# A graph layer and a mixture of experts on one core: block numbers loaded elsewhere, one-hots made a step ahead, W3's split moved, the expert loop written out

## What is computed

```python
def _L0_gnn_ref(x, edge_index, edge_attr, W1, b1, W2, b2, W3, b3, W4, b4, gamma, beta):
    src, dst = (edge_index[0], edge_index[1])
    edge_feat = jnp.concatenate([x[src], x[dst], edge_attr], axis=-1)
    h = mish(edge_feat @ W1 + b1)                # mish(x) = x * tanh(softplus(x))
    messages = mish(h @ W2 + b2)
    agg = jax.ops.segment_sum(messages, dst, num_segments=x.shape[0])
    u = mish(jnp.concatenate([x, agg], axis=-1) @ W3 + b3)
    y = x + (u @ W4 + b4)
    mu = jnp.mean(y, axis=-1, keepdims=True)
    var = jnp.mean(jnp.square(y - mu), axis=-1, keepdims=True)
    return (y - mu) * jax.lax.rsqrt(var + LN_EPS) * gamma + beta

def _L0_ffn_ref(hidden_states, gate_weight, w1, w2):
    gate_logits = x @ gate_weight.T
    top_vals, top_idx = jax.lax.top_k(gate_logits, 2)
    routing_w = jax.nn.softmax(top_vals, axis=-1)
    h = jax.nn.silu(jnp.einsum('td,efd->tef', x, w1))
    h_mean = jnp.einsum('tef,te->ef', h, mask) / counts[:, None]   # per expert
    y_mean = jnp.einsum('ef,edf->ed', h_mean, w2)
    return jnp.einsum('tk,tkd->td', routing_w, y_mean[top_idx])

x = x + _L0_gnn_ref(_layernorm(x), edge_index, edge_attr_64, ...)
x = x + _L0_ffn_ref(_layernorm(x)[None], gate_weight, w1, w2)[0]
```

## Time and profile before

| | us |
|---|---|
| median of 3 runs | 1254.94 (1253.52 to 1257.24) |
| the profiled execution | 1255.11 |
| its span, first to last instruction | 1253.5 |
| PE, DVE, ACT, POOL busy | 1084.6, 958.0, 837.7, 713.5 |
| mean granted TensorE clock | 0.929 |

### The profile page before, as it was taken

One profiled execution on the slowest core, in us unless ns is written; L12 is line 12 of the kernel. 1 busy time (PEld: TensorE's weight loads), 2 busy tenths in 40 slices (PEclk: granted clock), 3 DMA queues, 4 the chain that ended last, 5 costly groups with the idle time before them and its releaser, 6 DMA issues. The chain is left out here.

```text
span 1253.5 us, 19768 instructions
## 1 busy us (share of the span) xinstructions
PE 1084.6 (87%) x5651; PEld 884.2 (71%) x5652; DVE 958.0 (76%) x1678; ACT 837.7 (67%) x1025; POOL 713.5 (57%) x574
## 2 busy tenths in 40 slices
PE   3993999999999999999999999996389985668974
PEld 2772788787778778878777877885267764658862
DVE  6651799898989989989989999998548875733366
ACT  3212889989988998998998988897045441523342
...
GB/s 167 276 89 153 143 121 130 125 125 125 129 126 122 127 128 121 129 126 123 129 125 126 124 126 129 119 149 1 23 46 42 33 58 82 205 76 127 134 130 179
DMA packets 129763, 148.72 MB, mean 119 GB/s; under 512 B 73253, under 2 KB 81862, under 8 KB 129597
## 3 DMA queue, kind: packets, MB, share of 16 engines
...
## 5 line engine op out<-in xcount | busy, mean ns | idle before, releaser
L907 PE MATMUL ps<-W2h,w1l_w3l 128*128 128x512 f32 x1264 | 426.6, 398 | 0.0
L778 POOL DMA_INDIRECT gath<-dst_table,idx_sl x158 | 265.2, 1679 | 48.6 <-issue 47.1
L771 POOL DMA_INDIRECT gath<-src_table,idx_sl x158 | 207.9, 1316 | 126.1 <-PE ps L902 86.0
L907 PEld LDWEIGHTS ps<-W2h,w1l_w3l 128*128 128x128 f32 x1264 | 227.3, 189 | 38.6
L907 PE MATMUL ps<-W2l,w1l_w3l 128*128 128x512 f32 x632 | 248.2, 393 | 0.0
L845 DVE TENSOR_TENSOR agg<-agg,ps 125x512 f32 x166 | 114.0, 687 | 76.5 <-issue 47.7
L785 POOL TENSOR_TENSOR msg_lo<-act,msg_hi 128x512 fp32r<-128x512 f32 x79 | 144.2, 1825 | 35.3 <-DVE msg_hi L891 35.3
L907 PEld LDWEIGHTS ps<-W2l,w1l_w3l 128*128 128x128 f32 x632 | 119.0, 188 | 27.2
L802 ACT ACTIVATE act<-ps 128x1024 f32<-128x1024 f32 x79 | 81.2, 1027 | 74.8 <-PE ps L939 74.8
L902 PE MATMUL ps<-ident,gath 128*128 128x128 f32 x632 | 99.0, 282 | 34.8 <-DVE agg L845 18.4
L902 PEld LDWEIGHTS ps<-ident,gath 128*128 128x128 f32 x632 | 73.6, 142 | 62.5 <-DVE agg L845 35.3
...
## 6 DMA issues: line engine op xcount, KB each, us to landing
...
```

The source lines that it names most:

```text
L771: pool.indirect_dma_start(out=gath[:, k, j, :], out_offset=None, in_=src_table[:, :], in_offset=bass.IndirectOffsetOnAxis(ap=idx_sl[:, p % ...
L778: pool.indirect_dma_start(out=gath[:, k, j, :], out_offset=None, in_=dst_table[:, :], in_offset=bass.IndirectOffsetOnAxis(ap=idx_sl[:, p % ...
L907: return nc.tensor.matmul(ps_2[:, p % 2, j, :], part[:, p % 2, d, j * P:(j + 1) * P], weights[:, d, :], start=False, stop=last)
```

## The change

Four things are changed.

1. In the edge stage `value_load` is taken out of `add_sums`. The number for the first addition is loaded behind the second activation's product (L875 before) and ahead of L879, that for the second addition behind the lo part of h (L884) and ahead of L887, so L887, L891 and L852 now stand between it and the addition.
2. The one-hot at that place in VectorE's order is that of f = s - 3 instead of m = s - 4, in three buffers (OH) instead of two.
3. W3's lo parts: VectorE makes four (0 to 3), one each in the steps PAIRS + 4 to PAIRS + 7, GpSimd four (4 to 7) in step PAIRS + 3. Before, VectorE made six, two each in PAIRS + 2 to PAIRS + 4, and GpSimd two.
4. The expert loop is written out for all 35 tiles on every engine. `row_sl` and `carrier` are gone, the gathers take their rows from `row_i` directly, and `xg` has four buffers (XG). The routing weights (`weights()`) are computed ahead of the loop. `reach`, `hs` and `spread_hm` lie on the memory of `bias_r`, which the expert stage does not read.

The edge stage's part of the diff, and the buffers:

```diff
         act_parts = {PAIRS: (0, 1, 2, 3), PAIRS + 1: (4, 5, 6, 7)}
-        dve_parts = {PAIRS + 2: (0, 1), PAIRS + 3: (2, 3), PAIRS + 4: (4, 5)}
-        pool_parts = {PAIRS + 3: (7, 6)}
+        dve_parts = {PAIRS + 4: (0,), PAIRS + 5: (1,), PAIRS + 6: (2,), PAIRS + 7: (3,)}
+        pool_parts = {PAIRS + 3: (4, 5, 6, 7)}
         hi_order = act_parts[PAIRS] + act_parts[PAIRS + 1]
...
-            def add_sums(p, j):
-                b = dve.value_load(block_i[0:1, p * 2 + j:p * 2 + j + 1], min_val=0, max_val=BLOCKS - 1)
+            def visit_block(p, j):
+                return dve.value_load(block_i[0:1, p * 2 + j:p * 2 + j + 1], min_val=0, max_val=BLOCKS - 1)
+
+            def add_sums(p, j, b):
                 row = agg[:, bass.ds(b, 1), :].rearrange("p a d -> p (a d)")
                 dve.wait_ge(S["sum_ps"], p + 1)
                 if p * 2 + j > 0:
...
                 if visited(o):
-                    add_sums(o, 1)
+                    add_sums(o, 1, second)
...
-                if visited(m):
-                    if m >= 2:
-                        dve.wait_ge(S["sum_ps"], m - 1)
-                    nc.vector.tensor_tensor(onehot[:, m % 2], iota_n[:].unsqueeze(1).to_broadcast([P, 2, NE]),
-                                            dloc[:, 2 * m:2 * m + 2].unsqueeze(2).to_broadcast([P, 2, NE]), ALU.is_equal).then_inc(S["onehot_ready"], 1)
+                if visited(f):
+                    if f >= OH:
+                        dve.wait_ge(S["sum_ps"], f - OH + 1)
+                    nc.vector.tensor_tensor(onehot[:, f % OH], iota_n[:].unsqueeze(1).to_broadcast([P, 2, NE]),
+                                            dloc[:, 2 * f:2 * f + 2].unsqueeze(2).to_broadcast([P, 2, NE]), ALU.is_equal).then_inc(S["onehot_ready"], 1)
...
+                if visited(m):
+                    first = visit_block(m, 0)
                 if exists(p):
                     dve.wait_ge(S["exp1"], p + 1)
                     nc.vector.tensor_scalar(a1, a1, EXP_MAX, 1.0, ALU.min, ALU.add).then_inc(S["inc1"], 1)
                 if visited(m):
-                    add_sums(m, 0)
+                    add_sums(m, 0, first)
                 if exists(r):
                     dve.wait_ge(S["h_hi"], r + 1)
                     nc.vector.tensor_tensor(hTl[:, r % 2], h, f32(hTh[:, r % 2]), ALU.subtract).then_inc(S["h_lo"], 1)
+                if visited(m):
+                    second = visit_block(m, 1)
...
                     o = sums(m)
                     for j in range(2):
                         for lo, part in enumerate((msg_hi, msg_lo)):
-                            ins = nc.tensor.matmul(o[0:NE, j, :], onehot[:, m % 2, j, :], part[:, bass.ds(slots[j], 1), :].rearrange("p a n -> p (a n)"),
+                            ins = nc.tensor.matmul(o[0:NE, j, :], onehot[:, m % OH, j, :], part[:, bass.ds(slots[j], 1), :].rearrange("p a n -> p (a n)"),
...
-        carrier = sb("f_carrier", [1, 2])
-        row_sl = sb("row_sl", [P, 2, 1], I32)
-        xg = sb("xg", [P, 2, HID])
+        xg = sb("xg", [P, XG, HID])
...
-        hs = sb("hs", [P, 2, FFN])
+        hs = over_bias("hs", [P, 2, FFN], 0)
```

The expert loop's part (ScalarE's is rewritten in the same way):

```diff
-            def step(i, c):
-                g, k, _ = tile(i, c + 2)
-                if within(g, RT):
-
-                    pool.wait_ge(S["row_ready"], g + 1)
-                    need(pool, S["xgT_ps"], g - 1)
-                    pool.wait_ge(S["carried"], g + 1)
-
-                    nc.gpsimd.tensor_tensor(carrier[:, 0:1], carrier[:, 1:2], carrier[:, 1:2], ALU.add).then_inc(S["carried"], 1)
-                    pool.indirect_dma_start(out=xg[:, k, :], out_offset=None, in_=xl_scr[:, :],
-                                            in_offset=bass.IndirectOffsetOnAxis(ap=row_sl[:, k, 0:1], axis=0)).then_inc(gathered[k], 16)
-
-            nc.gpsimd.memset(carrier[:], 0.0).then_inc(S["carried"], 1)
-            steps(pool, step, FIRST, LAST, LO, HI, UNROLL)
+            pool.wait_ge(S["rows_ready"], 1)
+            for t in range(RT):
+                if t >= XG:
+                    pool.wait_ge(S["xgT_ps"], t - XG + 1)
+                pool.indirect_dma_start(out=xg[:, t % XG, :], out_offset=None, in_=xl_scr[:, :],
+                                        in_offset=bass.IndirectOffsetOnAxis(ap=row_i[:, t:t + 1], axis=0)).then_inc(gathered[t % XG], 16)
...
-            def step(i, c):
-                g, k, used = tile(i, c + 3)
-                if within(g, RT):
-
-                    need(dve, gathered[k], used * 16)
-                    nc.vector.tensor_copy(row_sl[:, k, :], row_i[:, bass.ds(g, 1)]).then_inc(S["row_ready"], 1)
-                if isinstance(i, int) and c == FIRST + 1:
-
-                    weights()
-                m, km, _ = tile(i, c - 3)
-                if within(m, RT):
-
-                    e = dve.value_load(expert_i[0:1, bass.ds(m, 1)], min_val=0, max_val=E - 1)
+            weights()
+            for t in range(-1, RT + 3):
+                m, n = t - 3, t + 1
+                if m >= 0:
+                    e = dve.value_load(expert_i[0:1, m:m + 1], min_val=0, max_val=E - 1)
                     cols = hsum[:, :, bass.ds(e, 1)].rearrange("p f a -> p (f a)")
                     dve.wait_ge(S["sum_ps"], m + 1)
                     need(dve, S["summed"], m)
-                    nc.vector.tensor_tensor(cols, cols, ps_s[:, km, 0:FC], ALU.add).then_inc(S["summed"], 1)
-                n, kn, _ = tile(i, c + 1)
-                if within(n, RT):
-
+                    nc.vector.tensor_tensor(cols, cols, ps_s[:, m % 2, 0:FC], ALU.add).then_inc(S["summed"], 1)
+                if n < RT:
                     dve.wait_ge(S["xgT_hi"], n + 1)
-                    nc.vector.tensor_tensor(xgTl[:, kn, :], ps_t[:, kn, :], f32(xgTh[:, kn, :]), ALU.subtract).then_inc(S["xgT_lo"], 1)
-
-            steps(dve, step, FIRST, LAST, LO, HI, UNROLL)
+                    nc.vector.tensor_tensor(xgTl[:, n % 2, :], ps_t[:, n % 2, :], f32(xgTh[:, n % 2, :]), ALU.subtract).then_inc(S["xgT_lo"], 1)
...
-            def step(i, c):
-                t, k, _ = tile(i, c)
-                if within(t, RT):
-                    e = pe.value_load(expert_i[0:1, bass.ds(t, 1)], min_val=0, max_val=E - 1)
-                n, kn, used = tile(i, c + 1)
-                if within(n, RT):
-
-                    pe.wait_ge(gathered[kn], used * 16 + 16)
+            for t in range(-1, RT + 2):
+                m, n = t - 2, t + 1
+                if 0 <= t < RT:
+                    e = pe.value_load(expert_i[0:1, t:t + 1], min_val=0, max_val=E - 1)
+                if n < RT:
+                    pe.wait_ge(gathered[n % XG], (n // XG + 1) * 16)
                     need(pe, S["xgT_lo"], n - 1)
                     for q in range(KC):
-                        ins = nc.tensor.transpose(ps_t[:, kn, q * P:(q + 1) * P], xg[:, kn, q * P:(q + 1) * P], ident[:])
+                        ins = nc.tensor.transpose(ps_t[:, n % 2, q * P:(q + 1) * P], xg[:, n % XG, q * P:(q + 1) * P], ident[:])
                     ins.then_inc(S["xgT_ps"], 1)
-                m, km, _ = tile(i, c - 2)
-                if within(m, RT):
-
+                if 0 <= m:
                     pe.wait_ge(S["h_act"], m + 1)
                     need(pe, S["summed"], m - 1)
                     for f in range(FC):
-                        ins = nc.tensor.matmul(ps_s[:, km, f:f + 1], hs[:, km, f * P:(f + 1) * P], valid[:, bass.ds(m, 1)], start=True, stop=True)
+                        ins = nc.tensor.matmul(ps_s[:, m % 2, f:f + 1], hs[:, m % 2, f * P:(f + 1) * P], valid[:, m:m + 1], start=True, stop=True)
                     ins.then_inc(S["sum_ps"], 1)
-                if within(t, RT):
-
+                if 0 <= t < RT:
+                    k = t % 2
...
-
-            steps(pe, step, FIRST, LAST, LO, HI, UNROLL)
-
```

36 lines of the change are left out of this document (17 added, 19 removed).

## The result

The changed kernel takes **1197.4 us** (median of 4 runs, 1195.2 to 1197.9) against 1254.5 us: ratio 0.954, 95% interval 0.952 to 0.956. Predicted were 1200, range 1192 to 1214. The profiled execution took 1197.5 us, its span is 1195.9, so the trace of before (span 1253.5) and this one differ by 57.6 us.

The account below looks back on a forecast made before the run. The prediction took VectorE to set the edge stage's period, partly by fetching block numbers while TensorE waits. Its terms, -34 - 11 - 10 = -55, gave 1200 us from a profiled 1255.11, range 1192 to 1214.

Parts of the forecast that it names:

- Term 1: Edge stage: moving the two block number loads ends TensorE's 0.50 us wait per period; -34 us, bounds -36 and -24.
- The witness periods: Edge stage: the last two periods with gathered tiles, at 8.98 us, taken as the period after the change.
- the 1 us for hiccups: Edge stage: taken off 35 us for small hiccups that count fully once TensorE is the bound.
- The witnesses named: Edge stage signs: period 8.98 to 9.0, no VectorE wait or issue time before additions; load above 0.9 us means upper bound.
- The upper bound of 0.15 us a period: Edge stage: a slow load behind L884 sticks out of its 1.22 us cover by 0.15 us at most.
- Terms 2 and 3: Drain: one-hots a step ahead -9.4, W3's split -2.3, one hold +1; together -11 us, bounds -14 and -5.
- The 1 us charged for one more held operation: Drain: GpSimd's doubled W3 parts would hold a VectorE operation once more; 1 us.
- Term 4: Expert loop: no copies or carrier, four buffers, tiles 2.33 us apart instead of 2.66; -10 us, bounds -11.5 and +0.
- Another limit at 9.2 us or more: Rival, edge stage: a gather, ScalarE or GpSimd holds the period at 9.2 to 9.25; 1217 us, chance 0.12.
- A starving written-out loop: Rival, expert loop: seven instruction refills at 1.5 us each use up the 10 us; 1210 us, chance 0.08.
- The drain gives nothing: Rival, drain: GpSimd's parts hold VectorE throughout; 1206 to 1211 us, chance 0.04.
- Loads that wait for everything ahead of them: Rival, edge stage: both loads stick out fully wherever they stand, period 9.99 us; 1270 us, chance 0.03.

Follow-up runs that it names:

- a1: The kernel before with only the two block number loads moved behind the long products: 1220.5 us, ratio 0.972.
- a2: The changed kernel with each block number load put back right ahead of its addition: 1231.4 us, ratio 0.981.
- a3: The changed kernel with the second load one place further back, behind the messages' hi part (0.69 us): 1198.3 us, ratio 0.954.
- a4: The kernel before, loads unmoved, with GpSimd's half of msg_lo ahead of its gathers of the second table, which start later: 1219.3 us (one run).
- c3: The changed kernel with GpSimd's W3 parts waiting for VectorE's last msg_lo, and GpSimd's msg_lo ahead of the second table's gathers: 1195.0 us, ratio 0.952.
- b3: The kernel before with only the one-hots a step ahead, in three buffers: 1246.2 us, ratio 0.994.
- b4: The changed kernel with W3's split as before, six parts on VectorE and two on GpSimd: 1199.8 us, ratio 0.956.
- b1: The kernel before with only the written-out expert loop and its four gather buffers: 1244.1 us, ratio 0.991.
- b2: The changed kernel with two gather buffers in place of four, the expert loop still written out: 1203.3 us, ratio 0.959.
- a5: The changed kernel with VectorE's block numbers of the edge stage replaced by constants, so no load is left there: 1194.4 us, ratio 0.952.

## Why the prediction was right, and where its steps were not

- **Term 1, the loads, -34.** Measured -34.9 (after), -35.3 (a1), +34.0 (a2). The witness periods without gathers, 8.98 us, gave the right period for the ones with gathers, and the 1 us for hiccups was not needed. The witnesses named all hold: issue time before additions gone but for 0.4 us, loads below 0.9 us. The *reason* was half right. "I cost both loads at nothing where they land" rested on cover; a3 and a4 show that the loads are short there because they no longer meet the second adding gather, and c3 shows for the first load that cover hides a held one too (for the second, behind L889, no run shows it). The prediction named the gather as running beside the slow load, and took its witness from it, but didn't ask beside which gather the moved loads would land. That they land where a load is short was not foreseen, and in so far luck. The upper bound of 0.15 us a period was never touched.
- **Terms 2 and 3, the drain, -11 (-9.4, -2.3, +1).** Measured -11.9. One-hots alone 9.0 (b3), the split 2.9 to 3.4 (after against b3, b4 against after), where -2.3 + 1 was put. A step was put at "some 2.4 us, about what TensorE's four matmuls take"; it is 2.23, and VectorE's alone: TensorE's clock was granted at its higher level from about 848.5 us, behind two sums that ran back to back (a sum's matmul then shows 0.40 instead of 0.63 us), and it waits 1.0 us a step. The 1 us charged for one more held operation is the step that was wrong: held in the drain after are the last msg_lo (1.75 us) and the one-hot ahead of it (1.11 at 842.06), and both stand in the trace of before too (1.75 at 879.01, 1.12 at 869.98), so the change added none. TensorE's first sum came 1.9 us earlier (41.4 for 43.3 behind pair 77), where 2.3 was put, and the steps with one part instead of two are shorter by the rest.
- **Term 4, the expert loop, -10.** Measured -11.9 by the table, of which 0.8 is the clock at the start, so -11.1 from the fourth tile on (b1's medians: -10.7). The undisturbed tile was 2.33 in the earlier trace rows and is 2.30, so that 31 tiles give 11.1 us where 10.2 was put; the 0.5 us for the first gather are 0.4; the 0.7 us for fetching the longer program have no counterpart in the trace: 30 tiles run at 2.30 us without one exception. The prediction didn't say what share the buffers have; b2 shows 7.5 us for them and 3.0 to 3.6 for the copies, the carrier and the loop on the chip.
- **The rivals.** Another limit at 9.2 us or more: no, TensorE is busy in every microsecond of the stage. A starving written-out loop: no; the queue of instruction fetches moved 49 packets where there were 44, and no tile pauses. By the Trainium skill's rule that the prediction quotes (Runtime: NRT & Kernel Launch, Instruction fetch mechanics) refills are mostly hidden, and the trace agrees: tiles 2.30 us apart throughout. The drain gives nothing: no. Loads that wait for everything ahead of them: no, a5 finds 0.006 us a period left in them.
- **The sum.** -55 against -57.1 of the medians. What the terms left out (+0.9 ahead, -1.0 between, +1.2 behind) cancels to 1.1 us and is of the size by which those stages move anyway; the excess over -55 comes from the terms: 0.9 us in the edge stage, 0.9 in the drain, 1.9 in the loop, 0.8 of it the clock's. Taken off as a precaution were 1 us for hiccups, 1 for a hold and 0.7 for fetching, and none of these came. The parts measured one by one add up as well, in medians: -35.3 (a1), -10.7 (b1), -8.6 (b3) and -2.4 (b4) make -57.0.
